# Transposes of the last two preparations moved to the DMA queue, their projections set two tiles behind the aggregation

## The chip, the cores and the metric

One core of one Trainium2 chip runs the whole program in one launch. The metric is the device time in microseconds. Three runs of the kernel before took 705.76, 706.26 and 706.27 us; the median is 706.26.

## The reference

Four layers on 2048 nodes with 256 features and one 0/1 adjacency matrix. Each layer's result is added to its input and normalised per row (mean and variance over the 256 features).

```python
x = layernorm(x + adj @ (x @ W0) + b0)
# attention, 4 heads: e = leaky_relu(src_i + dst_j) + adj;  att = softmax(e)
x = layernorm(x + mean_heads(att @ (x @ W1)))
# two convolutions: conv(x) = relu(x @ Wa + adj @ (x @ Wb) + b)
h = conv1(x);  x = layernorm(x + relu(conv2(h) + h))
# graph convolution: relu(adj_norm @ x @ W3), adj_norm = d^-1/2 (adj + I) d^-1/2
x = layernorm(x + relu(adj_norm @ (x @ W3)))
```

## The kernel before

Rows are handled in T = 16 tiles of P = 128; D = 256. Every float32 operand of TensorE is split into two float16 parts, hi and lo, and a product is made of such parts: a projection is six matmuls (three pairs of parts, two halves of the contraction), an aggregation two per tile of columns (the adjacency is exact in bf16, the projected features have hi and lo).

There are five **preparations**, k = 0 to 4 (k = 0 the first layer, 1 the attention's sources, 2 and 3 the two convolutions, 4 the graph convolution), and four **aggregations**, a = 0 to 3, for k = 0, 2, 3, 4. While aggregation a runs, preparation of the next k is woven into it. This text speaks of k = 3 woven into a = 1 ("convolution 2") and k = 4 woven into a = 2 ("the graph convolution"). A preparation of a tile goes through all engines:

- VectorE, `stages`: sum of the aggregated tile out of PSUM (line 779; 776 in the last aggregation), for k = 4 also residual, statistics (793, 800, 804), normalise (759); then `split` writes the hi part into the ring `xs` of R = 4 slots (827 for k = 3, 829 for k = 4).
- GpSimd: for k = 4 the inverse deviation (1109, 1111); `prep_lo` writes the lo part (1116).
- The tile is turned. Tiles 0 to 10 (`EARLY` = 11) by a DMA transpose that SP issues (lines 292 to 298; SP waits for each to land before the next, line 298). Tiles 11 to 15 by four TensorE transposes (`transpose`, 504) into the banks 4 and 5 of PSUM, evacuated by ScalarE (336).
- TensorE, `project` (541): six matmuls into bank 6 or 7 (`prep_bank`), 512 columns wide for k = 3, 256 for k = 4.
- ScalarE, `take_p`: the hi part of the projected features into `pset` (345; for k = 4 also 344). VectorE, `take`: lo part and own term (741, 744).

The order on TensorE is written out by hand. An aggregation works the row tiles 0 to 3 in four banks together (`group0`), then the tiles 4 to 15 one after the other (`rest`, lines 586 to 602): 16 steps j of two matmuls (550 hi, 551 lo) into one bank. Round t of `rest` first waits for the sum four tiles back (591). The projection of tile t - 5 of the next preparation is put ahead of step j = 14 of tile t. After the last tile, `tail` (604 to 614) does the transposes 11 to 15 and the projections 11 to 15, between pieces of the next aggregation's `group0`.

The order on VectorE is `first_sums` (tiles 0 to 3) and `other_sums` (835 to 877). Round t of `other_sums` interleaves the early stages of tile t (sum first) with the late ones of tile t - 1 (normalise, split), then the take of tile t - 4. So the split of tile t - 1 always stands behind the sum of tile t.

```python
                for n in range(max(len(early), len(late_))):
                    for st in early[n:n + 1] + late_[n:n + 1]:
                        st()
```

`pset` holds hi and lo of every tile in rows of PW = D + 2 float16: 1032 bytes to a tile, lo at byte 516, and hi's column D is the column of ones that gives the degrees in a = 0. The attention's `val` has rows of the same PW per head and tile, hi and lo in two arrays, which the change leaves alone.

Of the kernel before, what the change touches and what calls it, by code (L numbers as in the profile page):

```python
# [7 lines left out]
def graph_stack(nc, x_in, adj_in, w0_in, b0_in, w1_in, a_in, w2a_in, b1_in, w2b_in, b2_in, w3_in, out):  # L8
# [23 lines left out]
    R = 4  # L32
# [19 lines left out]
    with ctx:  # L52
# [62 lines left out]
        PSET = T * 2 * PW // 2  # L115
        pset = [part(arena, (s * PSET, (s + 1) * PSET), F16, "p (t q f) -> p t q f", t=T, q=2) for s in range(2)]
# [39 lines left out]
        s_td = sem("s_td")  # L156
# [57 lines left out]
        EARLY = T - R - 1  # L214

        def by_pe(k, t):

            return k * T + t if k < 2 else 2 * T + (k - 3) * (T - EARLY) + t - EARLY

        def conv_turned(t):  # L220

            return s_tc[t % 2], 16 * (t // 2 + 1)

        def prep_bank(k, u):

            return ps[:, 4 + u if k == 2 else 6 + u % 2, :]

        def by_dma(k, t):

            return 16 * ((k - 3) * EARLY + t + 1)  # L230

# [5 lines left out]
        def _(sp):  # L237
# [43 lines left out]
            for t in range(T):  # L281
                if t >= 2:
                    sp.wait_ge(*conv_turned(t - 2))
                if t % R == 0:
                    if t // R < SLOTS - 1:
                        sp.wait_ge(s_mm, (GROUPS - 1) * (T - 1) + T - SLOTS + t // R + 1)
                    else:
                        sp.wait_ge(s_z, GROUPS * BANKS)
                sp.wait_ge(s_lo, 2 * T + t + 1)
                sp.dma_start_transpose(xt[:, t, :].rearrange("p (c i) -> p c i", c=2 * K2),  # L290
                                       xs[:, t % R, :, :].rearrange("p q f -> p (q f)")).then_inc(s_tc[t % 2], 16)
            for k in (3, 4):
                sp.wait_ge(s_w, k * T)
                for t in range(EARLY):
                    sp.wait_ge(s_lo, k * T + t + 1)
                    sp.dma_start_transpose(xt[:, t, :].rearrange("p (c i) -> p c i", c=2 * K2),
                                           xs[:, t % R, :, :].rearrange("p q f -> p (q f)")).then_inc(s_td, 16)
                    sp.wait_ge(s_td, by_dma(k, t))
# [20 lines left out]
        def _(act):  # L319
# [6 lines left out]
            def split_hi(k, t, u, src, ready):  # L326
                ready(act)
                if k == 2 and t >= R:
                    act.wait_ge(*conv_turned(t - R))
                elif k == 0 and t >= R:  # L330
                    act.wait_ge(s_t, t - R + 1)
# [6 lines left out]
            def take_p(k, t, u):  # L338
                act.wait_ge(s_w, t + (k * T + 1))
                b = prep_bank(k, u)  # L340
                dst = pset[k % 2][:, at(t, 1), 0, 0:D].rearrange("p a f -> p (a f)")
# [148 lines left out]
            for k in (3, 4):  # L490
                tiles(act, 0, EARLY - EARLY % R, lambda t, u: take_p(k, t, u))
                for t in range(EARLY - EARLY % R, EARLY):
                    take_p(k, t, t % R)
                lagged(k, EARLY)
# [3 lines left out]
        def _(pe):  # L498
# [11 lines left out]
            def project(k, t, u):  # L510
                if k == 0 and isinstance(t, int) and t == 0:
                    pe.wait_ge(s_wl, 1)
                if k == 2:
                    pe.wait_ge(*conv_turned(t))
                elif k > 2 and not (isinstance(t, int) and t >= EARLY):
                    pe.wait_ge(s_td, by_dma(k, t))
# [4 lines left out]
                elif k == 2:  # L521
# [23 lines left out]
            def agg_step(a, k, it, bank, j, done):  # L545
# [4 lines left out]
                nc.tensor.matmul(ps[:, bank, 0:width], lhs, pp[:, j, 0, 0:width], start=(j == 0), stop=False)  # L550
                ins = nc.tensor.matmul(ps[:, bank, 0:D], lhs, pp[:, j, 1, 0:D], start=False, stop=(j == T - 1))  # L551
# [34 lines left out]
            def rest(a, knext, ready):  # L586
# [3 lines left out]
                def one(t, u):  # L590
                    pe.wait_ge(s_sum, t + (a * T - R + 1))
                    prep = knext is not None and not (isinstance(t, int) and t == R)
                    for j in range(T):
# [4 lines left out]
                        if j == (T - 2 if knext in (3, 4) else T // 2 + 2) and prep:  # L598
                            project(knext, t - R - 1, (u - 1) % R)
                        agg_step(a, k, t, u, j, j == T - 1)  # L600
                one(R, 0)
                tiles(pe, R + 1, T, one)

            def tail(k, a):

                e = T - R
# [578 lines left out]
```

## Time and profile before

| | us |
|---|---|
| runs, median (lowest to highest) | 706.26 (705.76 to 706.27) |
| the profiled execution | 704.71 |
| its span | 702.6 |
| mean granted clock of TensorE | 0.999 |
| TensorE busy | 686.1 (98%) |
| VectorE busy | 527.8 (75%) |
| ScalarE busy | 393.6 (56%) |
| GpSimd busy | 148.7 (21%) |

By stage, in us from the span's start: the first layer and the attention's set-up to about 134, the attention to 472, preparation k = 2 with its first sums to 507, a = 1 with k = 3 to 585, a = 2 with k = 4 to 654, a = 3 to the end. Times in the profile are microseconds unless marked ns. PE is TensorE, PEld its weight load, DVE VectorE, ACT ScalarE, POOL GpSimd, SP the queue that issues DMAs; a q behind the name is the engine's sequencer, L541 is line 541. A matmul's duration holds the way through the array, so the distance from one start to the next is its cost. `ring_hl` is the buffer that the turned tiles `xt` lie in, `ring_a` that of `xs`, `arena` holds `pset`, own and hidden terms.

### The profile page before, as it was taken

How to read it: one execution, taken by the hardware profiler on the slowest of the kernel's cores; microseconds unless marked ns; L12 is line 12 of the kernel's file. 1: busy time of each engine (PE TensorE's matmuls, PEld its weight loads, DVE VectorE, ACT ScalarE, POOL GpSimd, SP SyncE). 2: the span in 40 equal slices, each digit the busy share in tenths (PEclk: the TensorE clock that was granted, in tenths of full speed). 3: DMA queues.
4: the chain of work that ended last, by engine and by line, in shares of the span. 5: the costliest groups of instructions: out<-in, count | busy, mean ns of one | idle time of the engine just before them, and what ended most of it. 6: DMA issues, size and time to landing. Idle time of an engine off the chain costs nothing.

```text
span 702.6 us, 16657 instructions
## 1 busy us (share of the span) xinstructions
PE 686.1 (98%) x5962; PEld 567.2 (81%) x5962; DVE 527.8 (75%) x985; ACT 393.6 (56%) x525; POOL 148.7 (21%) x239
## 2 busy tenths in 40 slices
PE   6989999999999999999999999999999999999996
PEld 4878854688888888888888888876677778888885
DVE  5888646999898989989899898998432325874564
ACT  7554146888989889798898989643100020223000
POOL 4966422000100000000000000654011102432222
PEclk9999999999999999999999999999999999999999
DMA  8986001000303012030300303013121000210011
GB/s 327 413 311 261 0 3 60 1 1 31 62 31 61 0 42 49 30 60 0 80 10 30 60 0 60 2 29 70 23 46 31 8 1 16 39 30 2 31 49 42
DMA packets 33147, 42.17 MB, mean 60 GB/s; under 512 B 21776, under 2 KB 27856, under 8 KB 30928
## 3 DMA queue, kind: packets, MB, share of 16 engines
q1 hardware_dynamic: 30528, 33.73, 14.7%
q0 software_dynamic: 2016, 7.34, 5.6%
q8 instruction: 28, 0.46, 0.3%
q10 hardware_dynamic: 560, 0.52, 0.2%
q14 instruction: 15, 0.12, 0.1%
HBM read 27.13 MB, written 2.13 MB: 42 GB/s over the span
## 4 chain that ended last, share of the span: by engine, by line
PE 89%; DVE 7%; ACT 1%; issue 1%; DMA 1%; POOL 1%; DVEq 0%; SPq 0%; POOLq 0%; ACTq 0%
PE ps L550 15%; PE ps L551 15%; PE ps L692 14%; PE ps L694 14%; PE ps L693 14%; PE ps L541 9%; PE ps L642 5%; DVE ring_hl L986 2%; DVE ring_a L981 2%; PE ps L504 1%; DMA x<-in_x 1%; DVE x L759 1%; POOL ring_a L1116 0%; DVE stat L753 0%; PE ps L533 0%
## 5 line engine op out<-in xcount | busy, mean ns | idle before, releaser
L694 PE MATMUL ps<-arena,ring_hl 128*128 (+1 forms) x1024 | 279.6, 273 | 0.0
L692 PE MATMUL ps<-arena,ring_hl 128*128 (+1 forms) x1024 | 278.9, 272 | 0.4 <-DVE ring_hl L986 0.4
L693 PE MATMUL ps<-arena,ring_hl 128*128 (+1 forms) x1024 | 278.6, 272 | 0.0
L550 PE MATMUL ps<-arena,adj 128*128 128x256 f16 (+1 forms) x1024 | 230.5, 272 | 0.5 <-issue 0.5
L551 PE MATMUL ps<-arena,adj 128*128 128x256 f16 x1024 | 230.6, 273 | 0.0
L981 DVE SCALAR_TENSOR_TENSOR ring_a<-rho,gam,ring_a 128x1024 f32<-128x1024 f32 x128 | 163.8, 1280 | 18.0 <-ACT ring_a L435 18.0
L986 DVE TENSOR_TENSOR ring_hl<-ring_a,ring_hl 128x1024 f16<-128x1024 f32 x128 | 156.6, 1223 | 6.0 <-ACT ring_hl L449 5.9
L449 ACT ACTIVATE ring_hl<-ring_a 128x1024 f16<-128x1024 f32 x128 | 135.2, 1056 | 44.3 <-PE ps L694 31.0
L435 ACT ACTIVATE ring_a<-adj,shift 128x1024 f32<-128x1024 bf16 x128 | 145.6, 1138 | 0.0
L550 PEld LDWEIGHTS ps<-arena,adj 128*128 (+1 forms) x1024 | 99.9, 98 | 18.2 <-issue 0.7
L551 PEld LDWEIGHTS ps<-arena,adj 128*128 (+1 forms) x1024 | 99.5, 97 | 16.1
L692 PEld LDWEIGHTS ps<-arena,ring_hl 128*128 128x128 f16 x1024 | 100.0, 98 | 12.8 <-DVE ring_hl L986 0.9
L693 PEld LDWEIGHTS ps<-arena,ring_hl 128*128 128x128 f16 x1024 | 99.1, 97 | 13.7
L694 PEld LDWEIGHTS ps<-arena,ring_hl 128*128 128x128 f16 x1024 | 99.5, 97 | 13.1
L1139 POOL DMA_DIRECT2D x<-y x14 | 12.3, 880 | 308.3 <-ACT y L464 308.3
L345 ACT ACTIVATE arena<-ps 128x256 f16<-128x256 f32 (+1 forms) x48 | 18.5, 385 | 96.1 <-PE ps L541 95.8
L741 DVE SCALAR_TENSOR_TENSOR arena<-ps,w 128x256 f32<-128x256 f32 (+1 forms) x32 | 13.5, 422 | 56.1 <-ACT arena L345 56.0
L336 ACT ACTIVATE ring_hl<-ps 128x512 f16<-128x512 f16 (+1 forms) x42 | 25.0, 597 | 42.0 <-PE ps L504 42.0
L1111 POOL TENSOR_TENSOR rstd<-veps,neghalf 128x1 f32<-128x1 f32 x64 | 44.5, 696 | 5.0
L642 PE MATMUL ps<-w,ring_hl 128*128 128x512 f16 x192 | 42.7, 379 | 0.6 <-DVE arena L964 0.6
L1116 POOL TENSOR_TENSOR ring_a<-x,ring_a 128x256 f16<-128x256 f16 (+1 forms) x38 | 31.9, 842 | 43.4 <-DVE ring_a L829 39.9
L759 DVE TENSOR_SCALAR x<-total,mv,rstd 128x256 f32<-128x256 f32 (+1 forms) x48 | 19.8, 411 | 26.3 <-POOL rstd L1111 26.3
(91 smaller groups left out, 553.7 us busy)
## 6 DMA issues: line engine op xcount, KB each, us to landing
arena<-in_adj SPq DMA_DIRECT2D x16, 1024.0 KB, 9.1
x<-y POOLq DMA_DIRECT2D x14, 512.0 KB, 5.2
rho<-s_scratch SPq DMA_DIRECT2D x8, 512.0 KB, 3.7
out_x<-x SPq DMA_DIRECT2D x16, 128.0 KB, 1.7
x<-in_x SPq DMA_DIRECT2D x3, 512.0 KB, 6.9
arena<-in_L_gnn_W SPq DMA_DIRECT2D x1, 1024.0 KB, 16.4
arena<-in_L_gnn_a SPq DMA_DIRECT2D x1, 1024.0 KB, 19.4
rho<-in_L_gnn_W SPq DMA_DIRECT2D x2, 512.0 KB, 10.4
```

Source lines behind the costliest of these rows:

```text
L435: nc.scalar.activation(ring_a[:, jt % SLOTS, :], adj[:, jt, q * CH:(q + 1) * CH], ACT.Exp, bias=shift[:, at(h, 1), jt]).then_inc(s_e, 1)
L449: nc.scalar.activation(ring_hl[:, jt % SLOTS, 0], ring_a[:, jt % SLOTS], ACT.Copy).then_inc(s_ah, 1)
L541: ins = nc.tensor.matmul(bank[:, 0:width], xpart(a, kk), w[:, b, kk, :], start=(n == 0), stop=(n == len(steps) - 1))
L550: nc.tensor.matmul(ps[:, bank, 0:width], lhs, pp[:, j, 0, 0:width], start=(j == 0), stop=False)
L551: ins = nc.tensor.matmul(ps[:, bank, 0:D], lhs, pp[:, j, 1, 0:D], start=False, stop=(j == T - 1))
L642: ins = nc.tensor.matmul(ps[:, 2 * u + half, :], xtt[:, (a * K2 + kk) * P:(a * K2 + kk + 1) * P], w1[:, b, kk, half * 512:(half + 1) * 512 ...
L692: nc.tensor.matmul(acc, hi, v_hi, start=(jt == 0), stop=False)
L693: nc.tensor.matmul(ps[:, b, 0:D], hi, v_lo, start=False, stop=False)
L694: ins = nc.tensor.matmul(acc, lo, v_hi, start=False, stop=(jt == T - 1))
L981: nc.vector.scalar_tensor_tensor(a, rho[:, q, :], gam[:, at(h, 1), jt], a, op0=ALU.max, op1=ALU.mult)\
L986: nc.vector.tensor_sub(ring_hl[:, jt % SLOTS, 1], ring_a[:, jt % SLOTS], ring_hl[:, jt % SLOTS, 0])\
L1111: nc.gpsimd.tensor_tensor(rstd[:, slot:slot + 1], veps[:, slot:slot + 1], neghalf[:, 0:1], ALU.pow)\
```

## The change

All 16 tiles of k = 3 and 4 are turned by DMA, two semaphores in turn as k = 2 already had them, SP waiting for the landing two tiles back. A projection of k > 1 uses banks 4 to 7 and waits for the take four tiles back. The places of the projections on TensorE (tile: projected tile, step j) and of the takes on VectorE are written in two tables; from tile 9 (k = 3) and 13 (k = 4) on, tile t projects tile t - 2 at j = 14. The tail has two projections and no transposes. `rest` and `other_sums` are unrolled for these preparations instead of looping from tile 8. The rows of `pset` are 2 x 264 + 2 x 256 = 1040 bytes, lo at byte 528.

```diff
 
-        PSET = T * 2 * PW // 2
-        pset = [part(arena, (s * PSET, (s + 1) * PSET), F16, "p (t q f) -> p t q f", t=T, q=2) for s in range(2)]
+        LOW = D + 8
+        PSET = T * (LOW + D) // 2
+        pset = [part(arena, (s * PSET, (s + 1) * PSET), F16, "p (t f) -> p t f", t=T) for s in range(2)]
...
 
-        EARLY = T - R - 1
-
...
 
-            return k * T + t if k < 2 else 2 * T + (k - 3) * (T - EARLY) + t - EARLY
-
-        def conv_turned(t):
-
-            return s_tc[t % 2], 16 * (t // 2 + 1)
+            return k * T + t
+
+        def turned(k, t):
+
+            return s_tc[t % 2], 16 * ((k - 2) * T // 2 + t // 2 + 1)
+
+        PLACES = {3: {5: [(0, T - 2)], 6: [(1, 2), (2, T - 2)], 7: [(3, 2), (4, T - 2)], 8: [(5, 2), (6, T - 2)],
+                      **{t: [(t - 2, T - 2)] for t in range(9, T)}},
+                  4: {5: [(0, T - 2)], 6: [(1, T - 2)], 7: [(2, T - 2)], 8: [(3, JH), (4, T - 2)], 9: [(5, T - 2)],
+                      10: [(6, JH), (7, T - 2)], 11: [(8, T - 2)], 12: [(9, JH), (10, T - 2)],
+                      **{t: [(t - 2, T - 2)] for t in range(13, T)}}}
+        TAKES = {3: {5: [0], 6: [1, 2], 7: [3, 4], 8: [5, 6], **{t: [t - 2] for t in range(9, T)}},
+                 4: {4: [0], 5: [1], 6: [2, 3], 7: [4, 5], **{t: [t - 2] for t in range(8, T)}}}
...
 
-            return ps[:, 4 + u if k == 2 else 6 + u % 2, :]
-
-        def by_dma(k, t):
-
-            return 16 * ((k - 3) * EARLY + t + 1)
+            return ps[:, 4 + u if k > 1 else 6 + u % 2, :]
...
 
-            for t in range(T):
-                if t >= 2:
-                    sp.wait_ge(*conv_turned(t - 2))
-                if t % R == 0:
-                    if t // R < SLOTS - 1:
-                        sp.wait_ge(s_mm, (GROUPS - 1) * (T - 1) + T - SLOTS + t // R + 1)
-                    else:
-                        sp.wait_ge(s_z, GROUPS * BANKS)
-                sp.wait_ge(s_lo, 2 * T + t + 1)
-                sp.dma_start_transpose(xt[:, t, :].rearrange("p (c i) -> p c i", c=2 * K2),
-                                       xs[:, t % R, :, :].rearrange("p q f -> p (q f)")).then_inc(s_tc[t % 2], 16)
-            for k in (3, 4):
-                sp.wait_ge(s_w, k * T)
-                for t in range(EARLY):
+            for k in (2, 3, 4):
+                if k > 2:
+                    sp.wait_ge(s_w, k * T)
+                for t in range(T):
+                    if t >= 2:
+                        sp.wait_ge(*turned(k, t - 2))
+                    if k == 2 and t % R == 0:
+                        if t // R < SLOTS - 1:
+                            sp.wait_ge(s_mm, (GROUPS - 1) * (T - 1) + T - SLOTS + t // R + 1)
+                        else:
+                            sp.wait_ge(s_z, GROUPS * BANKS)
...
                     sp.dma_start_transpose(xt[:, t, :].rearrange("p (c i) -> p c i", c=2 * K2),
-                                           xs[:, t % R, :, :].rearrange("p q f -> p (q f)")).then_inc(s_td, 16)
-                    sp.wait_ge(s_td, by_dma(k, t))
+                                           xs[:, t % R, :, :].rearrange("p q f -> p (q f)")).then_inc(s_tc[t % 2], 16)
...
                     pe.wait_ge(s_wl, 1)
-                if k == 2:
-                    pe.wait_ge(*conv_turned(t))
-                elif k > 2 and not (isinstance(t, int) and t >= EARLY):
-                    pe.wait_ge(s_td, by_dma(k, t))
+                if k > 1:
+                    pe.wait_ge(*turned(k, t))
...
                     pe.wait_ge(s_ev, BANKS * (GROUPS - 1) + 1 + t)
-                elif k == 2:
+                elif k > 1:
...
                 lhs = adj[:, j, at(it * P, P)]
-                nc.tensor.matmul(ps[:, bank, 0:width], lhs, pp[:, j, 0, 0:width], start=(j == 0), stop=False)
-                ins = nc.tensor.matmul(ps[:, bank, 0:D], lhs, pp[:, j, 1, 0:D], start=False, stop=(j == T - 1))
+                nc.tensor.matmul(ps[:, bank, 0:width], lhs, pp[:, j, 0:width], start=(j == 0), stop=False)
+                ins = nc.tensor.matmul(ps[:, bank, 0:D], lhs, pp[:, j, LOW:LOW + D], start=False, stop=(j == T - 1))
...
                             transpose(knext, t - R - 1, (u - 1) % R)
-                        if j == (T - 2 if knext in (3, 4) else T // 2 + 2) and prep:
+                        if j == T // 2 + 2 and prep and knext < 3:
                             project(knext, t - R - 1, (u - 1) % R)
+                        for n, place in PLACES.get(knext, {}).get(t, []) if isinstance(t, int) else []:
+                            if place == j:
+                                project(knext, n, n % R)
...
                 one(R, 0)
-                tiles(pe, R + 1, T, one)
+                if knext in PLACES:
+                    for t in range(R + 1, T):
+                        one(t, t % R)
+                else:
+                    tiles(pe, R + 1, T, one)
...
 
-                e = T - R
-                plan = [([], e - 1, None), ([0, 1, 2], e, e - 1), ([3, 4], e + 1, e), ([5, 6], e + 2, e + 1),
-                        ([7, 8], e + 3, e + 2), ([9, 10], None, e + 3), (list(range(11, T)), None, None)]
-                for js, tt, tp in plan:
+                for js, tp in ((range(0, 5), T - 2), (range(5, 10), T - 1), (range(10, T), None)):
                     group0(a, k, js)
-                    if tt is not None:
-                        transpose(k, tt, tt % R)
...
                         dve.wait_ge(s_t, t + (k * T - R + 1))
-                    elif k == 3 and isinstance(t, int) and t < R:
-                        dve.wait_ge(*conv_turned(t + T - R))
-                    elif isinstance(t, int) and (t < R or t >= EARLY + R):
-                        dve.wait_ge(s_t, by_pe(*((k, t - R) if t >= R else (k - 1, t + T - R))) + 1)
+                    elif t < R:
+                        dve.wait_ge(*turned(k - 1, t + T - R))
                     else:
-                        dve.wait_ge(s_td, by_dma(k, t - R))
+                        dve.wait_ge(*turned(k, t - R))
...
                             lines[t][s - (t - 1)]()
-                for n, st in enumerate(lines[3][1:]):
-                    if n + 1 == len(lines[3]) - len(stages(a, k, 3, 3)[1]) and k is not None:
-                        take(k, 0, 0)
+                for st in lines[3][1:]:
...
                         late_ = []
-                    if k is not None and not (isinstance(t, int) and t == R and a > 0):
+                    if k == 1:
                         late_.append(lambda: take(k, t - R, u))
+                    for n in TAKES[k].get(t, []) if k in TAKES else []:
+                        late_.append(lambda n=n: take(k, n, n % R))
...
                             st()
-                peeled = max(len(fill), 1)
+                peeled = T - R if k in TAKES else max(len(fill), 1)
...
                 if k is not None:
-                    for t in range(T - R, T):
+                    for t in range(T - (R if k == 1 else 2), T):
```

Not shown: the same change of names and indices in ScalarE's `split_hi` and `take_p`, in VectorE's `take` and in GpSimd's memset of the ones; ScalarE's part for k = 3 and 4 becomes a loop of `take_p` over the 16 tiles.

## Rows read from the trace of the kernel before

**Rows 1.** The page's busy times: engine, us, share of the span, instructions.

```profile
PE 686.1 (98%) x5962; PEld 567.2 (81%) x5962; DVE 527.8 (75%) x985; ACT 393.6 (56%) x525; POOL 148.7 (21%) x239
```

**Rows 2.** The chain of waits in convolution 2: start us, us, what.

```profile
528.31 1.29 PE ps L541 x6
...
533.14 1.29 PE ps L541 x6
```

**Rows 3.** The timeline of two tile starts, last aggregation: start us, us, engine, line.

```profile
679.07 0.27 PE L550 MATMUL ps<-arena,adj 128*128 128x256 f16 x1
...
679.50 0.48 DVE L776 SCALAR_TENSOR_TENSOR arena<-ps,dis,arena 128x256 f32 x1 [1.70 <-PE ps L551]
...
682.60 0.27 PE L550 MATMUL ps<-arena,adj 128*128 128x256 f16 x1
```

**Rows 4.** The chain of waits, a tile turned on TensorE in the tail.

```profile
566.70 0.22 PE ps L504 x4
```

**Rows 5.** The timeline of one preparation in convolution 2, DVE, POOL and SP.

```profile
526.02 0.41 DVE L779 TENSOR_TENSOR arena<-ps,arena 128x256 f32<-128x256 f32 x1
526.35 0.28 DVE L827 TENSOR_SCALAR ring_a<-arena 128x256 f16<-128x256 f32 x1
...
526.83 0.67 POOL L1116 TENSOR_TENSOR ring_a<-arena,ring_a 128x256 f16<-128x256 f16 x1 [4.15 <-DVE ring_a L827]
527.57 1.19 SPq L296 DMA_TRANSPOSE ring_hl<-ring_a  x1
```

**Rows 6.** The chain of waits, graph convolution's first projection.

```profile
590.11 2.43 DMA ring_hl<-ring_a
...
592.58 0.83 PE ps L541 x6
```

**Rows 7.** The timeline of DVE and POOL in the graph convolution's preparation.

```profile
598.99 0.41 DVE L779 TENSOR_TENSOR arena<-ps,arena 128x256 f32<-128x256 f32 x1
...
618.84 0.41 DVE L759 TENSOR_SCALAR x<-total,mv,rstd 128x256 f32 x1 [0.47 <-POOL rstd L1111]
...
621.01 0.18 DVE L804 BATCH_NORM_AGGREGATE mv<-stat 128x2 f32<-128x6 f32 x1
...
622.12 0.41 DVE L759 TENSOR_SCALAR x<-total,mv,rstd 128x256 f32 x1 [0.47 <-POOL rstd L1111]
622.44 0.42 DVE L786 SCALAR_TENSOR_TENSOR arena<-arena  x1
622.78 0.41 DVE L829 TENSOR_SCALAR ring_a<-total,mv,rstd 128x256 f16<-128x256 f32 x1
...
623.38 0.67 POOL L1116 TENSOR_TENSOR ring_a<-x,ring_a 128x256 f16<-128x256 f16 x1 [1.30 <-DVE ring_a L829]
```

**Rows 8.** The timeline of a projection and its takes, graph convolution.

```profile
600.97 0.82 PE L541 MATMUL ps<-w,ring_hl 128*128 128x256 f16 x6
601.62 0.27 PE L550 MATMUL ps<-arena,adj 128*128 128x256 f16 x1
...
602.01 0.47 ACT L344 ACTIVATE arena<-ps,dis2w 128x256 f32 x1 [3.35 <-PE ps L541]
602.38 0.47 ACT L345 ACTIVATE arena<-ps,disw 128x256 f32 x1
...
631.50 0.47 ACT L345 ACTIVATE arena<-ps,disw 128x256 f16<-128x256 f32 x1
...
632.27 0.48 DVE L744 SCALAR_TENSOR_TENSOR arena<-ps,disw,arena 128x256 f32 x1 [0.81 <-ACT arena L345]
```

**Rows 9.** The 22 transposes of line 296, issue to landing.

```profile
DMA to landing us min/median/max: 2.4/2.4/4.3
```

**Rows 10.** Busy times by stretch, the attention's head 0 and head 2: us (matmuls).

```profile
150.00:200.00 50.00, 50.00 (x458) 44.58 (x456) 46.10 (x47) 43.74 (x48) 2.04 (x2) 1.00 0.15 33
...
300.00:350.00 50.00, 50.00 (x459) 44.20 (x457) 43.72 (x53) 44.23 (x54) 3.44 (x4) 1.00 0.21 44
```

**Rows 11.** Busy times by stretch, first layer: stretch, length, PE first, PEclk third last.

```profile
42.00:50.00 8.00, 5.74 (x59) 4.84 (x57) 6.69 (x18) 2.87 (x4) 5.74 (x7) 1.00 0.69 253
```

More of the change, by code:

```diff
@@ L155, in graph_stack @@
         s_t, s_xt = sem("s_t"), sem("s_xt")
-        s_td = sem("s_td")
         s_tc = [sem(f"s_tc{i}") for i in range(2)]
@@ L328, in split_hi @@
                 if k == 2 and t >= R:
-                    act.wait_ge(*conv_turned(t - R))
+                    act.wait_ge(*turned(2, t - R))
                 elif k == 0 and t >= R:
@@ L340, in take_p @@
                 b = prep_bank(k, u)
-                dst = pset[k % 2][:, at(t, 1), 0, 0:D].rearrange("p a f -> p (a f)")
+                dst = pset[k % 2][:, at(t, 1), 0:D].rearrange("p a f -> p (a f)")
                 src = b[:, D:2 * D] if k in (2, 3) else b[:, 0:D]
@@ L490, in _ @@
             for k in (3, 4):
[L491 to L494, printed above, removed]
+                tiles(act, 0, T, lambda t, u: take_p(k, t, u))
         @block.tensor
@@ L736, in take @@
                 dve.wait_ge(s_ph, t + ((k - (k > 1)) * T + 1))
-                hi = pset[k % 2][:, at(t, 1), 0, 0:D].rearrange("p a f -> p (a f)")
-                lo = pset[k % 2][:, at(t, 1), 1, 0:D].rearrange("p a f -> p (a f)")
+                hi = pset[k % 2][:, at(t, 1), 0:D].rearrange("p a f -> p (a f)")
+                lo = pset[k % 2][:, at(t, 1), LOW:LOW + D].rearrange("p a f -> p (a f)")
                 ot = tile_of(own, t)
@@ L1073, in _ @@
             nc.gpsimd.memset(ident[:, :], 0.0).then_inc(s_id0, 1)
-            nc.gpsimd.memset(pset[0][:, :, 0, D:D + 1], 1.0).then_inc(s_one, 1)
+            nc.gpsimd.memset(pset[0][:, :, D:D + 1], 1.0).then_inc(s_one, 1)
             pool.wait_ge(s_id0, 1)
```

## The prediction, made before the result was known

> **What bounds the kernel now.** I read the page's busy times first. TensorE is busy 98% of the span [rows 1]. Then the chain of waits in the stretch the diff touches: convolution 2 and the graph convolution, some 507 to 654 us. It is TensorE alone, tile after tile, 4.83 us apart in convolution 2 [rows 2]; a tile without a projection takes 682.60 - 679.07 = 3.53 us for its 32 aggregation matmuls, 16 pairs of 0.22 [rows 3], so a convolution projection costs 1.30, and one of the graph convolution 601.62 - 600.97 = 0.65 [rows 8]. TensorE has next to no idle time to win there. What can be won is work taken off it; what can be lost is a new wait. So I asked of each moved projection when its transposed tile lands.
>
> **What is taken off.** Before, tiles 11 to 15 of both preparations are turned on TensorE: four transposes to a tile, 40 in all. Four take 0.22 us of the chain [rows 4], so ten tiles give back 2.2 us. ScalarE loses ten evacuations; it isn't on the chain and this is worth nothing. Ten more transposes go to SP's queue, 1.19 us each to issue [rows 5]; tiles come over 4 us apart, the queue hides them, and SP's next work, the output stores, comes only in the last aggregation. Four banks instead of two: a projection waits for the take four tiles back, which VectorE has long made; worth nothing, and without that slack the second projection of tiles 6 to 8 would wait for the first one's take, some 1.5 us behind it [rows 8]. The old tail began each bank of the next layer with 3 rows, the new one with 5, so its fourth bank asks for the last sum later: I give that 0.4 us, one VectorE sum.
>
> **The chain that the new places make, convolution 2.** Call E the moment TensorE begins tile t. VectorE's round t-1 begins with the sum of tile t-1, which waits for the aggregation that ended at E; the split of tile t-2 stands behind that sum. So the tile that is projected in tile t can't be split before E. Step by step:
> - TensorE's new tile to VectorE's sum: 679.50 - 679.07 = 0.43 [rows 3].
> - Sum to split: 526.35 - 526.02 = 0.33; split to GpSimd's low part: 0.48; that to SP's issue: 0.74 [rows 5].
> - Issue to landing 2.43, landing to first matmul 0.04 [rows 6].
>
> The sum is 4.45 us after E. TensorE gets to place 14 after 14 pairs, 14/16 of 3.53 = 3.09 us. It waits 1.36 us, and since the aggregation's last two pairs are queued behind the wait, the tile's sum, VectorE's next round and the next tile start late too: nothing of it is caught up. Tiles 9 to 15 have this form: 7 x 1.36 = 9.5 us. Tiles 5 to 7 project what was split a round earlier and wait for nothing; tile 8 projects two, 3.09 + 1.30 = 4.39, and waits 0.1. In the tail, tile 14 comes after 20 pairs (4.41), just in time.
>
> **The same for the graph convolution.** Here the split is preceded by sum, normalise and max. VectorE's steps follow at 0.32 to 0.34 us (622.12, 622.44, 622.78), GpSimd starts 0.60 after the split [rows 7]. Chain: 0.43 + 0.33 + 0.32 + 0.34 + 0.60 + 0.74 + 2.43 + 0.04 = 5.23 us. Against 3.09 that is 2.14 for each of tiles 13, 14, 15: 6.4 us; in the tail 5.23 - 4.41 = 0.8.
>
> Earlier tiles depend on VectorE's lag. It comes out of its first four tiles late: it sums tile 4 at 598.99, when TensorE is near the end of tile 7 (600.97, rows 8). Its rounds are 622.12 - 618.84 = 3.28 us against TensorE's 3.53 + 0.65, so it gains 0.9 us a tile [rows 7]. I walked the two queues tile by tile with the steps above. Tile 8's second projection waits 0.3. The largest wait is tile 10: round 7 takes tile 5, whose projection stands at the end of tile 9. The take is ready 0.39 + 0.37 + 0.77 = 1.53 us after that projection ends [rows 8], or 1.09 after tile 10 starts (two pairs, 0.44, lie between). Only then come the take (0.48) and tile 7's statistics end; tile 7's normalise follows them by 622.12 - 621.01 = 1.11 [rows 7], its split by another 0.66, and 3.81 more to the matmul: 7.15 us after E (1.09 + 0.48 + 1.11 + 0.66 + 3.81). TensorE wants it at 3.09 + 0.65 = 3.74: 3.4 us of wait. The same walk gives 1.5 and 2.2 for the two projections of tile 12. Together 0.3 + 3.4 + 3.7 + 6.4 + 0.8 = 14.6 us.
>
> **Long landings.** The transposes land in 2.4 us in the middle and 4.3 at most [rows 9]. Until now a late one was covered by three tiles of lag; on this path it is paid in full. Bounds for the 15 awaited ones: none late, 0; all late, 15 x 1.9 = 28. Nearest is the median, so I take two late ones at 1.2: 2.3 us.
>
> **Padding.** The row of a tile goes from 1032 to 1040 bytes, the low half from byte 516 to 528. No row prices this. From above: six projection matmuls, whose operand rows start at multiples of 512 bytes, take 0.65 us, 109 ns each [rows 8], and an aggregation matmul 3.53/32 = 110.3 [rows 3]; if the padding brings one to the other, 2048 x 1.4 = 2.9 us. From below: in the attention head 0's value rows start at a multiple of 16 bytes and head 2's eight bytes past one, and 50 us hold 458 and 459 matmuls [rows 10]: nothing. A loss isn't excluded but no row hints at one: it adds no instruction. I take a gain of 1.7, because in the waiting tiles all but the last two pairs only lengthen the wait.
> The Trainium skill, SBUF — State Buffer, Specifications (TRN2), says that SBUF has 16-byte lines and that each cross to a new line pays a penalty; a 512-byte row off a line touches 33 of them instead of 32, which by that rule would be up to 3% of the aggregations, an estimated 7 us. The attention's two counts speak against it.
>
> **The sum.** Gains 2.2 + 0.4 + 1.7 = 4.3; losses 9.6 + 14.6 + 2.3 = 26.5; net +22.2. The profiled execution took 704.71 us (span 702.6, 2.1 around it), the median of the runs is 706.26, 1.55 above it; I add the net to the median: **728.5 us**.
>
> **Rivals.**
> - *The waits aren't there, faster.* For it: the rest of VectorE, GpSimd and SP is idle enough, and if the chain of steps were under 3.09 us the lag of two tiles would hide it all. Against: issue to landing alone is 2.43. Then 706.3 - 4.3 = 702.0. It decides for "faster" when the chain is below 3.09 us in convolution 2 and the last rounds of the graph convolution. Chance 0.07.
> - *Only the steady waits.* VectorE's lag falls otherwise than I walked it, and tiles 8, 10 and 12 of the graph convolution wait for little: 706.3 + 9.6 + 7.2 + 2.3 - 4.3 = 721.1. For it: that walk has the most steps. Chance 0.10.
> - *The clock falls.* TensorE would be idle about a fifth of these stretches. If its clock dropped to 1.2 GHz through 13 waiting tiles, the 3.09 before the projection becomes 6.18, which is 1.7 past the chain, and the 1.74 of work after it doubles: (1.7 + 1.7) x 13 = 45 us more, 773. Against: in the stretch 42 to 50 us TensorE is idle 2.26 of 8 us, 28% of it, and the clock still reads 1.00 [rows 11]. Chance 0.04.
> The Trainium skill, TensorE: Matmul & The Clock Gate, HAM oscillation, describes such a kernel, whose short bursts between waits on DMA each start at the low clock; this trace has no fallen clock beside such a gap.
> - *Gains and waits cancel*, within 0.2% of 706.3 (about 1.4 us, what a measurement of this kernel can tell from no change): it needs a chain some 1.2 us shorter and tile 10 without its wait. Chance 0.02.
>
> **How the numbers follow.** The forecast has 0.77. Its own bounds are 0 to 6 us of late landings, 0 to 2.9 of padding, and one or two us either way in the walk: about 723 to 734. To hold 8 in 10 I reach down to the steady-waits case: 719 to 735. Left out are the faster case, the cancelling case, the clock case and what is outside the bounds. Faster 0.07, same 0.02, slower 0.91.
>
> **What the profile would show.** TensorE's idle time before the projection's matmuls, released by the DMA ring_hl<-ring_a: about 26 us in some 17 waits, seven of them 1.4 us in convolution 2 and four about 2.1 in the graph convolution, one over 3; tiles 6.2 us apart in convolution 2. VectorE's sum 0.4 us behind each TensorE tile. No L504 after 100 us. The aggregation's 32 matmuls in 3.48 us if the padding tells, 3.53 if not. The forecast is wrong if the projection finds its tile landed, that is if the distance from a tile's start to the landing is under 3.1 us.

## The result and the profile after

The changed kernel takes **727.48 us** (median of 4 runs, 727.36 to 728.70) where the kernel before takes 706.11: a ratio of 1.0313 [1.0301, 1.0326] (in brackets the 95% interval). The ratio is the one on record; the quotient of the two medians is 1.0303. Below too the two differ by up to 0.001, so about 0.7 us of any difference between two versions hangs on which is taken. It was forecast slower, at 728.5 in a range of 719 to 735. The profiled execution took 727.37 us, its span is 724.9, 22.3 more than before. The page, busy times first, then the chain of waits by engine and line:

```profile
span 724.9 us, 16115 instructions
PE 687.5 (95%) x5922; PEld 566.3 (78%) x5922; DVE 526.9 (73%) x985; ACT 388.8 (54%) x515; POOL 148.9 (21%) x239
PE 78%; DVE 10%; DMA 6%; POOL 3%; issue 2%; ACT 1%; POOLq 0%; SPq 0%; ACTq 0%; DVEq 0%
```

TensorE has 40 matmuls fewer than in [rows 1] and is busy 95% instead of 98%; DMA now has 6% of the chain. Who waited for whom between 500 and 680 us (us in total, times, longest):

```profile
PEld ps L534 <- DMA ring_hl<-ring_a: 24.6, 16, 3.6
PE ps L534 <- DMA ring_hl<-ring_a: 20.1, 16, 3.3
```

L534 is the projection. Its weight load waits 24.6 us for transposes to land, in 16 waits. (The matmul's own figure is smaller because the array is still draining for part of the time. In the rest of the text a wait is the distance between two matmul starts less the 0.11 us of the first.) One tile of convolution 2, from the timeline; columns as in [rows 3]:

```profile
538.50 1.47 PE L534 MATMUL ps<-w2b,ring_hl 128*128 128x512 f16 x6 [1.00 <-DMA ring_hl<-ring_a]
...
540.24 0.27 PE L543 MATMUL ps<-arena,adj 128*128 128x256 f16 x1
...
540.44 0.42 DVE L774 TENSOR_TENSOR arena<-ps,arena 128x256 f32<-128x256 f32 x1 [3.81 <-PE ps L544]
...
540.78 0.28 DVE L820 TENSOR_SCALAR ring_a<-arena 128x256 f16<-128x256 f32 x1
...
541.26 0.67 POOL L1109 TENSOR_TENSOR ring_a<-arena,ring_a 128x256 f16<-128x256 f16 x1 [5.29 <-DVE ring_a L820]
...
542.00 1.19 SPq L295 DMA_TRANSPOSE ring_hl<-ring_a  x1
...
544.45 1.47 PE L534 MATMUL ps<-w2b,ring_hl 128*128 128x512 f16 x6 [0.99 <-DMA ring_hl<-ring_a]
```

```profile
542.00 2.40 DMA ring_hl<-ring_a
544.41 0.05 issue
```

This is the chain of the prediction, link by link (the second fence is the same tile in the chain of waits). The tile starts at 540.24, VectorE's sum follows 0.20 later, the split 0.34, the low part 0.48, the issue 0.74, the landing 2.40, the matmul 0.04: 4.21 us. TensorE was there after 3.06 (14 pairs of 0.218). Projections are 544.45 - 538.50 = 5.95 us apart where it was 4.83 [rows 2]. Seven such waits measure 1.15 to 1.17 us each. VectorE is idle 3.81 us before its sum: it is not short of time, it stands in the wrong place of its queue.

### The profile page after: what moved, and what is told of

Read it like the earlier page. It is cut to its first block, busy times and chain, and to the rows that moved or that the text cites. A ratio compares the mean times of both kernels' runs of the same rounds, so it can differ in the third digit from the quotient of the medians.

```text
span 724.9 us, 16115 instructions
## 1 busy us (share of the span) xinstructions
PE 687.5 (95%) x5922; PEld 566.3 (78%) x5922; DVE 526.9 (73%) x985; ACT 388.8 (54%) x515; POOL 148.9 (21%) x239
## 4 chain that ended last, share of the span: by engine, by line
PE 78%; DVE 10%; DMA 6%; POOL 3%; issue 2%; ACT 1%; POOLq 0%; SPq 0%; ACTq 0%; DVEq 0%
PE ps L687 14%; PE ps L689 14%; PE ps L688 14%; PE ps L543 11%; PE ps L544 11%; PE ps L534 9%; PE ps L637 5%; DMA ring_hl<-ring_a 5%; DVE ring_hl L979 2%; DVE ring_a L974 2%; POOL ring_a L1109 2%; DVE x L754 1%; PE ps L499 1%; POOL rstd L1104 1%; DVE arena L781 1%
## 5 line engine op out<-in xcount | busy, mean ns | idle before, releaser
L543 PEld LDWEIGHTS ps<-arena,adj 128*128 128x128 bf16 (+1 forms) x1024 | 100.7, 98 | 17.5 <-issue 0.9
L544 PEld LDWEIGHTS ps<-arena,adj 128*128 128x128 bf16 (+1 forms) x1024 | 100.8, 98 | 15.1
L774 DVE TENSOR_TENSOR arena<-ps,arena 128x256 f32<-128x256 f32 x32 | 13.2, 414 | 65.1 <-PE ps L544 65.1
L342 ACT ACTIVATE arena<-ps,dis2w 128x256 f32 x16 | 7.6, 473 | 71.1 <-PE ps L534 71.1
L534 PE MATMUL ps<-w,ring_hl 128*128 128x256 f16 x192 | 29.3, 294 | 14.4 <-DMA ring_hl<-ring_a 12.9
```

The costliest lines, as they stand in the source:

```text
L534: ins = nc.tensor.matmul(bank[:, 0:width], xpart(a, kk), w[:, b, kk, :], start=(n == 0), stop=(n == len(steps) - 1))
L543: nc.tensor.matmul(ps[:, bank, 0:width], lhs, pp[:, j, 0:width], start=(j == 0), stop=False)
L544: ins = nc.tensor.matmul(ps[:, bank, 0:D], lhs, pp[:, j, LOW:LOW + D], start=False, stop=(j == T - 1))
```

## Experiments

Each ratio is to the kernel before, run on the same chip beside it (it took 705.1 to 705.8 us there). Each diff is against the changed kernel unless it says otherwise, and is cut to the lines that matter: where places move, takes and tail move with them. The record also has the mean granted clock of every execution, a share of the full one: 0.991 to 0.994 in the four of the changed kernel, 0.996 to 0.999 in those of the kernel before beside the experiments. So a difference in time can be one of clock.

**1. Padding alone.** The kernel before with rows of 1040 bytes.

```diff
-        PSET = T * 2 * PW // 2
+        ROW = 2 * (D + 8) - 8
+        PSET = T * ROW // 2
...
-                ins = nc.tensor.matmul(ps[:, bank, 0:D], lhs, pp[:, j, 1, 0:D], start=False, stop=(j == T - 1))
+                ins = nc.tensor.matmul(ps[:, bank, 0:D], lhs, pp[:, j, D + 8:2 * D + 8], start=False, stop=(j == T - 1))
```

> The kernel before with the feature rows padded to 1040 bytes and nothing else. If the start of a row matters to TensorE (the changed kernel's trace has an aggregation pair at 0.218 to 0.219 us where the kernel before has 0.2205), the 1024 pairs save about 1.5 to 2.5 us: 703.6 to 704.6. If that difference comes from somewhere else in the change, the time stays within 0.3 us of 706.1.

Measured: 703.60 us, ratio 0.9978 [0.9965, 0.9990]: 1.5 us less. Busy times in a stretch of the last aggregation, matmuls in brackets behind PE; first the kernel before, then this one:

```profile
658.00:693.00 35.00, 35.00 (x320) 30.83 (x318) 20.30 (x73) 0.00 (x0) 9.60 (x26) 1.00 0.15 50
```

```profile
658.00:693.00 35.00, 35.00 (x323) 31.36 (x322) 20.08 (x73) 0.00 (x0) 9.60 (x26) 1.00 0.15 50
```

323 matmuls in place of 320 in 35 us. Over all starts of one pair behind another in the last three aggregations, a matmul costs 109.2 ns instead of 110.4, in the first 109.8 instead of 111.6. So the padding does speed TensorE, by 1536 x 1.2 + 512 x 1.8 ns = 2.8 us of work. The 1.5 us measured is less, with an interval of 0.7 to 2.5; the profiled execution also had a stretch of fallen clock (below), which takes about as much away as is missing. But the kernel before has executions with a lower clock too (on average it reads 0.998, this version 0.997), so the clock can be a part of the reason only, as far as is shown.

**2. All tiles by DMA, old places.** The two tables, the tail and the rows as before; transposes, banks and unrolling as in the change.

```diff
+        PLACES = {3: {t: [(t - 5, T - 2)] for t in range(5, T)},
+                  4: {t: [(t - 5, T - 2)] for t in range(5, T)}}
+        TAKES = {3: {t: [t - 4] for t in range(4, T)},
+                 4: {t: [t - 4] for t in range(4, T)}}
```

> The changed kernel with every projection and take put back where the kernel before has them (five tiles behind, five projections in the tail), unpadded rows; all tiles are still turned by DMA, four banks, rounds unrolled. If the new waits alone make the change slow: 706.1 less the 2.2 us of transposes, 703.5 to 704.3, with no TensorE wait for a transpose but the first of the graph convolution (0.6 us). If the ten more DMA transposes, the unrolled code or the banks cost something by themselves, it stays above 706.

Measured: 703.54 us, ratio 0.9977 [0.9966, 0.9987], 1.6 us less; the 2.2 us of transposes lie within it. TensorE waits for a transpose once, as in the kernel before:

```profile
PEld ps L536 <- DMA ring_hl<-ring_a: 0.7, 1, 0.7
```

So turning by DMA, four banks and unrolled rounds cost nothing that shows. What made the change slow is in the two tables with their tail (the rows aren't it: experiment 6 has the new rows and is as fast).

**3. Convolution 2 three tiles behind**, the graph convolution as changed.

```diff
-                      **{t: [(t - 2, T - 2)] for t in range(9, T)}},
+                      **{t: [(t - 3, T - 2)] for t in range(8, T)}},
...
-                for js, tp in ((range(0, 5), T - 2), (range(5, 10), T - 1), (range(10, T), None)):
+                for js, tp in TAIL[k]:
...
+        TAIL = {3: [(range(0, 5), T - 3), (range(5, 8), T - 2), (range(8, 11), T - 1), (range(11, T), None)],
```

> The changed kernel with convolution 2 alone projected three tiles behind (three projections in the tail); the graph convolution keeps its places. A tile more of lag gives the chain 4.8 us more, over the 1.36 it lacks: its seven waits of 1.27 and the 0.5 in the tail go, 727.5 - 9.4 = 718.1, and the graph convolution's waits stay at about 14. If the waits only move to other projections, less than 3 us is won.

Measured: 717.22 us, ratio 1.0181 [1.0161, 1.0201]: 1.3% of 706, 9.3 us, less than the changed kernel. The waits of convolution 2 make 8.6 us of it. Part of the rest can be clock: this version's executions take 715.3 and 716.5 us at a granted clock of 0.999 and 0.996, 718.0 and 719.8 at 0.991. The waits for transposes:

```profile
PEld ps L537 <- DMA ring_hl<-ring_a: 15.8, 9, 3.2
```

Nine instead of 16. The eight left besides the first projection's are the graph convolution's, and they stand as walked: tile 8, 10, 12 (two), 13, 14, 15 and the tail, here the timeline from tile 10 on.

```profile
617.16 0.83 PE L537 MATMUL ps<-w,ring_hl 128*128 128x256 f16 x6 [2.95 <-DMA ring_hl<-ring_a]
...
625.53 0.83 PE L537 MATMUL ps<-w,ring_hl 128*128 128x256 f16 x6 [1.21 <-DMA ring_hl<-ring_a]
...
629.61 0.83 PE L537 MATMUL ps<-w,ring_hl 128*128 128x256 f16 x6 [1.94 <-DMA ring_hl<-ring_a]
...
635.71 0.83 PE L537 MATMUL ps<-w,ring_hl 128*128 128x256 f16 x6 [1.78 <-DMA ring_hl<-ring_a]
641.82 0.83 PE L537 MATMUL ps<-w,ring_hl 128*128 128x256 f16 x6 [1.78 <-DMA ring_hl<-ring_a]
647.93 0.83 PE L537 MATMUL ps<-w,ring_hl 128*128 128x256 f16 x6 [1.79 <-DMA ring_hl<-ring_a]
654.03 0.83 PE L537 MATMUL ps<-w,ring_hl 128*128 128x256 f16 x6 [0.47 <-DMA ring_hl<-ring_a]
```

By distance of starts the eight are 1.06, 3.11, 1.37, 2.10, 1.95, 1.94, 1.95 and 0.63 us, 14.1 together.

**4. The graph convolution five tiles behind**, convolution 2 as changed.

```diff
-                  4: {5: [(0, T - 2)], 6: [(1, T - 2)], 7: [(2, T - 2)], 8: [(3, JH), (4, T - 2)], 9: [(5, T - 2)],
...
+                  4: {6: [(0, 4), (1, T - 2)], **{t: [(t - 5, T - 2)] for t in range(7, T)}}
```

> The changed kernel with the graph convolution alone put back to five tiles behind, its first projection a little later still; convolution 2 keeps two tiles. Its waits (some 14 us by the steps, 0.8 of them at the first projection) go: 727.5 - 14.4 = 713.1, less up to 1 us more if the two stretches at the low clock, which lie in this stage, go too. Convolution 2 still waits seven times 1.27 us. If VectorE's lag were the limit rather than the places, TensorE would wait for the same landings later and the time would stay over 720.

Measured: 710.48 us, ratio 1.0086 [1.0065, 1.0107], 16.0 us under the changed kernel. Its waits make 14.3 of that: the 14.1 of experiment 3, and 0.2 at the first projection, which waits 0.5 instead of 0.7. The changed kernel's two stretches of fallen clock (2.7 us, below) lie in this stage, and this trace has none there; that would make 17.0, within the interval of 1.5 us either way. Convolution 2 keeps seven waits of 1.15 to 1.17 us and one of 0.6 in the tail; the graph convolution has one of 0.5 left. With experiment 3, 9.3 + 16.0 = 25.3 us: that is the whole loss of 22.1 us and 3.2 more, about what the version of experiment 5 gains.

**5. Both.** Places of experiments 3 and 4 together, padded rows.

> The changed kernel with both preparations on places that the steps say need no wait: convolution 2 three tiles behind, the graph convolution five behind with its first projection at tile 6; all tiles by DMA, rows padded. If the waits are the whole loss and the three gains add up: before, less 2.2 (transposes), less some 2 (padding; it alone measured -1.5), less 0.4 to 1.0 (first wait of the graph convolution): a ratio to the kernel before of 0.992 to 0.995, 699.5 to 701.5 us where the kernel before takes 705.1. If something else of the change costs, it is over 702.

Measured: 702.04 us, ratio 0.9946 [0.9928, 0.9963], 3.8 us faster than the kernel before. The interval lies wholly under 1. The 702.04 us touch the 702 over which another cost was expected, but the kernel before took 705.83 beside them, not 705.1; the ratio is inside the expected range.

**6. Five behind in both, padded rows**: experiment 2 with the rows of the change.

> All tiles by DMA, every projection five tiles behind as in the kernel before, rows padded: the transposes' gain (0.9977 by itself) and the padding's (0.9978 by itself) together. If they add, 0.9955. Against the version with three and five tiles of lag (0.9946) it lacks only the 0.6 us at the first projection of the graph convolution and the 0.4 us behind the last sum, so 0.9955 to 0.9960. If the two gains overlap (both shorten TensorE's path, so they should not), it is over 0.997.

Measured: 702.15 us, ratio 0.9948 [0.9931, 0.9966]. The two gains add (0.9977 x 0.9978 = 0.9955, inside the interval). That it stands level with experiment 5 means that the half us at the graph convolution's first projection, and the one behind the last sum, can't be seen in the time.

**7. Split before the sum.** Two tiles behind as in the change; on VectorE, in convolution 2 alone, the split of tile t - 1 goes ahead of the sum of tile t.

```diff
-                        for st in early[n:n + 1] + late_[n:n + 1]:
+                        pair = (early[n:n + 1], late_[n:n + 1])
+                        for st in sum(pair[::-1] if k == 3 and n == 0 else pair, []):
```

> The changed kernel, projections still two tiles behind; only on VectorE in convolution 2, a round splits tile t-1 before the sum of tile t instead of behind it. If the queue order on VectorE is what ties the chain to the tile's start, the split comes a whole tile earlier, the seven waits of 1.27 us and the 0.5 behind them go and the ratio falls from 1.031 to about 1.018, as with three tiles of lag. If the distance from split to landing (3.7 us) alone were the cause, the waits would stay.

Measured: ratio 1.0188 [1.0173, 1.0203], as with three tiles of lag. VectorE's timeline shows the split (L820) done and the sum (L774) waiting behind it, and the projections 4.79 us apart:

```profile
541.72 0.28 DVE L820 TENSOR_SCALAR ring_a<-arena 128x256 f16<-128x256 f32 x1
...
543.25 1.46 PE L534 MATMUL ps<-w2b,ring_hl 128*128 128x512 f16 x6
...
545.18 0.42 DVE L774 TENSOR_TENSOR arena<-ps,arena 128x256 f32<-128x256 f32 x1 [3.18 <-PE ps L544]
...
548.04 1.46 PE L534 MATMUL ps<-w2b,ring_hl 128*128 128x512 f16 x6
```

Nothing changed but this order, and 8.8 us (1.25% of 706) are gone. So the lag of two tiles wasn't too short for the chain of split, low part and landing; it was too short for that chain behind a sum.

**8. Takes in step** with the projections, graph convolution.

```diff
-                 4: {4: [0], 5: [1], 6: [2, 3], 7: [4, 5], **{t: [t - 2] for t in range(8, T)}}}
+                 4: {5: [0], 6: [1], 7: [2, 3], 8: [4], 9: [5], 10: [6, 7], 11: [8], 12: [9, 10],
+                     **{t: [t - 2] for t in range(13, T)}}}
```

> The changed kernel, only VectorE's takes of the graph convolution moved one to three rounds later, into the round of the tile that projects them (take 5 from round 7 to 9). If take 5 holding round 7 makes the 3.3 us wait at tile 10, that wait falls to about 1.2, the 1.5 at tile 12's first projection goes and the 2.2 at its second falls to 1.5; the others stay: 4.7 us less, a ratio of about 1.025. If VectorE's own load makes these waits, they stay as they are.

Measured: ratio 1.0207 [1.0193, 1.0222], 7.5 us under the changed kernel (6.5 by the medians) where 4.7 were expected. The waits did what was said: 3.1 us fell to 1.17, 1.4 went, 2.1 fell to 1.28, the others of this stage stayed.

```profile
626.65 0.83 PE L535 MATMUL ps<-w,ring_hl 128*128 128x256 f16 x6 [1.00 <-DMA ring_hl<-ring_a]
...
630.81 0.82 PE L535 MATMUL ps<-w,ring_hl 128*128 128x256 f16 x6
...
633.64 0.82 PE L535 MATMUL ps<-w,ring_hl 128*128 128x256 f16 x6
...
636.89 0.28 PE L535 MATMUL ps<-w,ring_hl 128*128 128x256 f16 x1 [1.11 <-DMA ring_hl<-ring_a]
```

Summed, that is 4.1 us. The rest is near what the fallen clock takes from the changed kernel in this stage (below); this trace has none there, and the four executions read 0.995 to 0.998. The trace also has a wait of 1.5 us in convolution 2's tail where the changed kernel's has 0.45, behind a transpose that took 4.06 us to land; it is the slowest of the four. That this accounts for all of it is argued, not shown.

**9. Place 10 instead of 14**, convolution 2.

```diff
-                      **{t: [(t - 2, T - 2)] for t in range(9, T)}},
+                      **{t: [(t - 2, T - 6)] for t in range(9, T)}},
```

> The changed kernel, only the projections of convolution 2 from tile 9 on put ahead of step 10 instead of 14. The landing is tied to the tile's start, so TensorE waits 0.88 us longer in each of seven tiles (2.15 instead of 1.27) and does 4 pairs more behind the projection: 6.1 us more, a ratio of 1.040. If the waits were a matter of how much the queues or TensorE have to do, the place would matter little and the time stays within 1 us of the changed kernel.

Measured: ratio 1.0379 [1.0360, 1.0397], 4.7 us over the changed kernel where 6.1 were expected. In the stage itself the expectation holds: seven waits of 2.04 us, projections 565.52 - 558.68 = 6.84 us apart, against 5.95: 0.89 a tile.

```profile
558.68 1.47 PE L534 MATMUL ps<-w2b,ring_hl 128*128 128x512 f16 x6 [1.88 <-DMA ring_hl<-ring_a]
...
565.52 0.82 PE L534 MATMUL ps<-w2b,ring_hl 128*128 128x512 f16 x3 [1.88 <-DMA ring_hl<-ring_a]
```

Again the graph convolution shows no fallen clock in this trace, which the changed kernel's does.

**10. The change without padding.**

```diff
-        LOW = D + 8
+        LOW = PW
```

> The changed kernel with the rows as before, 1032 bytes. The aggregation matmul goes back from 109.2 to 110.4 ns, but in the ten waiting tiles all but the last two pairs are covered by the wait; what is paid is 0.4 us in the two stages, 0.5 in the last aggregation and 1.0 in the first: 1.9 us more than the changed kernel, a ratio of 1.034. If the padding were worth its full 2.8 us here too, 1.035; if nothing, 1.031.

Measured: ratio 1.0303 [1.0277, 1.0329]. That is no slower than the changed kernel's 1.0313, and 1.034 lies outside the interval: the expectation was missed. (By the medians this version is 22.1 us over the kernel before, the changed one 21.4.) In the trace the aggregation matmul is back at 110.4 ns and the seven waits are 0.03 us shorter, so what padding wins ahead of a wait the wait takes back. From the tail's wait to the end of the span, a stretch without any wait for a transpose, it takes 59.3 us instead of 58.9. The clock blurs the rest. Two executions of this version have 726.45 us at a granted clock of 0.998 and 0.999, the other two 729.07 at 0.993 and 729.18 at 0.991. The changed kernel's four are all at 0.991 to 0.994 and take 727.4 to 728.7. At like clock this version is 0.5 to 1.7 us slower, so the medians don't exclude the forecast 1.9 as clearly as the interval says; so few executions don't settle it.

**11 and 12. Where a row starts.** Padding alone again, rows of 1040 bytes, one profiled execution each. Both diffs are against experiment 1. In 11 the low half starts at byte 516; in 12 the low half at 8 and the high half at 520.

```diff
-                ins = nc.tensor.matmul(ps[:, bank, 0:D], lhs, pp[:, j, D + 8:2 * D + 8], start=False, stop=(j == T - 1))
+                ins = nc.tensor.matmul(ps[:, bank, 0:D], lhs, pp[:, j, D + 2:2 * D + 2], start=False, stop=(j == T - 1))
```

```diff
-                nc.tensor.matmul(ps[:, bank, 0:width], lhs, pp[:, j, 0:width], start=(j == 0), stop=False)
-                ins = nc.tensor.matmul(ps[:, bank, 0:D], lhs, pp[:, j, D + 8:2 * D + 8], start=False, stop=(j == T - 1))
+                nc.tensor.matmul(ps[:, bank, 0:width], lhs, pp[:, j, D + 4:D + 4 + width], start=(j == 0), stop=False)
+                ins = nc.tensor.matmul(ps[:, bank, 0:D], lhs, pp[:, j, 4:D + 4], start=False, stop=(j == T - 1))
```

> Padding alone, rows of 1040 bytes, but the low half at byte 516, four past a multiple of 16. In the kernel before, tiles j with hi at 0 and lo at 4 bytes past a multiple of 16 start their pair 0.2165 us apart and those with 8 and 12 past 0.225. If only 8 and 12 cost, every aggregation matmul takes 109.2 ns on average here, as with all rows at 0. If any start off a multiple costs, it takes about 109.8, halfway to the 110.4 of the kernel before.

> Padding alone, rows of 1040 bytes, the low half first at byte 8, the high half at byte 520: every operand row starts eight past a multiple of 16. If a start eight past costs by itself, an aggregation matmul takes 111 ns or more (the pairs of odd j before: 112.5). If the cost is in going from one start to another, or is none as in the attention's head 2, it takes 109.2.

Both have 323 matmuls in the stretch of experiment 1 and a mean of 109.2 ns, like rows at multiples of 16, though 12 has all its rows eight past one. First 11, then 12:

```profile
658.00:693.00 35.00, 35.00 (x323) 31.37 (x322) 20.35 (x73) 0.00 (x0) 9.62 (x26) 1.00 0.15 50
```

```profile
658.00:693.00 35.00, 35.00 (x323) 30.95 (x321) 20.34 (x73) 0.00 (x0) 9.61 (x26) 1.00 0.15 50
```

A start four or eight bytes past a multiple of 16 costs nothing here by itself. Taken by tile of columns in the last aggregation, a pair of matmuls costs 218.3 ns in even and odd tiles alike in experiments 1 and 11. In the kernel before it costs 216.4 in even ones (starts 0 and 4 past) and 224.8 in odd ones (8 and 12 past), in experiment 12, whose starts are all 8 past, 220.0 and 216.7. The Trainium skill, SBUF — State Buffer, Specifications (TRN2), has each cross to a new 16-byte line pay; by that, experiment 12's rows, which touch one line more, would be slower, and they aren't. In the first aggregation alone, whose high rows have 257 columns, 11 is slower than padding alone, 110.8 ns against 109.8. What the old layout of 1032 bytes does that these don't (a start twelve past, or the change from one start to the next) stays open.

## Why the prediction was right, and where it was not

**The bound and the new wait**: right. TensorE was the path, and the change put a wait for each landed tile on it. Experiments 3 and 4 take the waits away and with them the loss, experiment 7 shows that it hangs on the order of sum and split on VectorE, experiment 9 that it is tied to the tile's start.

**The chain of convolution 2**: right in form, 0.24 us too long. The step that was mis-sized is its first, tile start to sum: 0.43 us came from the last aggregation [rows 3], and it is 0.20 here. The wait is 1.16, not 1.36; the stage lost 8.1 us in seven waits and 0.45 in the tail, where 9.6 was forecast.

**The graph convolution**: forecast 0.3, 3.4, 1.5, 2.2, three of 2.1 and 0.8, 14.6 in all; without fallen clock they are 1.1, 3.1, 1.4, 2.1, three of 1.95 and 0.6, 14.1 in all (experiment 3). The only one off by more than 0.3 us is tile 8's. Experiment 8 shows that the long one came from the take that held VectorE's round, as the walk had it.

**Long landings**: 2.3 us were put in. The longest landing of the changed kernel's 32 took 3.2 us, not 4.3 as in [rows 9]:

```profile
DMA to landing us min/median/max: 2.4/2.4/3.2
```

One wait of the changed kernel's ends at a late landing, the 0.45 us in convolution 2's tail (first row); tile 8's ends at a usual one (second row) and is 1.06 to 1.09 us in all five padded traces with these places.

```profile
577.77 3.01 DMA ring_hl<-ring_a
...
612.01 2.41 DMA ring_hl<-ring_a
```

So 0.45 us is theirs, and it stands in the waits above. This term was 1.85 too large, and by chance: experiment 8's 4.06 us landing met the same wait. Four of the 32 took 2.8 to 3.2 us. Each of the four has a 16 KB fetch of instructions on another queue in its time, as have the four late ones of the kernel before (3.0 to 4.3 us). Here is the fetch beside the first row above, from the DMA queues between 577.7 and 580.8 us (packets, MB, share):

```profile
q8 instruction: 1, 0.02, 1.9%
```

One more transpose of the 32 has the end of such a fetch at its start and lands in 2.4. That the fetches make the others late isn't shown.

**The clock**: it had 0.04 as a rival and no term in the sum, and this is the step that failed. It did fall, twice for 3.4 us, each time at the end of one of the two longest waits (3.1 and 3.5 us; the second is tile 12's, in experiment 3's trace two waits of 1.4 and 2.1):

```profile
599.00:627.00 28.00, 23.67 (x215) 20.48 (x213) 19.57 (x67) 5.87 (x14) 10.95 (x24) 1.00 0.21 38
627.00:630.40 3.40, 3.40 (x19) 2.42 (x17) 1.30 (x5) 0.84 (x2) 0.80 (x3) 0.50 0.24 43
630.40:640.60 10.20, 6.91 (x63) 5.91 (x61) 5.02 (x17) 1.68 (x4) 3.03 (x7) 1.00 0.13 27
640.60:644.00 3.40, 3.37 (x16) 2.33 (x17) 1.02 (x4) 0.84 (x2) 0.00 (x0) 0.50 0.00 0
644.00:665.00 21.00, 16.25 (x146) 13.83 (x144) 9.65 (x35) 2.52 (x6) 5.66 (x12) 1.00 0.10 21
```

The clock stands third from the end: 0.50, the 1.2 GHz level, in the second and fourth stretch. From the first projection's wait to the tail's, this takes 665.34 - 599.51 = 65.8 us; in experiment 3, same places and no fallen clock, 653.29 - 590.13 = 63.2. So the clock cost 2.7 us in this execution, and the other three read no higher (0.991 to 0.993 against 0.994). It didn't stay down for the stage, as the rival had it. The rival's counter-argument, that a gap of 2.3 us left the clock at 1.00 [rows 11], was weak: in other executions that same gap is followed by 3.4 us at half clock.

**Gains**: transposes, 2.2 forecast, 1.6 [0.9 to 2.4] by themselves (experiment 2). Padding, 1.7 forecast for this kernel; alone 1.5 [0.7 to 2.5], inside the change not settled (experiment 10). The later wait for the last sum, 0.4 forecast: the kernel before waits 0.25 us there, at 638.01, and the changed kernel doesn't. I gave no more because the attention's rows showed nothing; that row could not speak for these, whose starts change from matmul to matmul.

The total came out 1.0 us from the forecast partly because errors cancel: waits with their late landings were put at 26.5 us and are 8.6 + 14.1 = 22.7, 3.8 too much, against 2.7 us of clock left out. That part is luck; the range holds without it.

## What to carry to other kernels

Before a consumer is moved nearer to its producer, add up the chain from the event that truly starts it, and that is not always the producer's own work: here an unrelated wait (the next tile's sum) stood ahead of the split in an in-order queue, and taking the split ahead of it is worth as much as a whole tile of lag. A wait on the bounding engine that recurs in every tile is paid in every tile. Distance cost nothing here: five tiles of lag in both preparations (experiment 6) are level with three and five (experiment 5). So take more lag than the chain needs, as long as buffers allow it. The best two versions measured keep the DMA transposes and the padding: 702.04 us, 0.9946 [0.9928, 0.9963] of the kernel before, with lags of three and five tiles, and 702.15 with five in both.

## What the runs showed of the hardware that was not expected

- **The same gap sometimes costs clock.** In the first layer TensorE stands idle 2.3 us from about 44 us on. Eight of the 14 traces then show 3.4 us at 1.2 GHz, 47.3 to 50.7 us here, others none. First padding alone, then the kernel before:

```profile
47.30:50.70 3.40, 3.40 (x24) 2.42 (x22) 2.77 (x7) 1.83 (x2) 2.37 (x4) 0.50 0.58 186
```

```profile
47.30:50.70 3.40, 3.40 (x39) 3.01 (x37) 2.91 (x7) 2.14 (x2) 2.45 (x3) 1.00 0.63 229
```

  24 matmuls instead of 39 in the same 3.4 us. Experiment 5's trace has two such stretches, at 18 us behind a gap of 1.8 and at 49, and a span of 701.2 us; that of experiment 6, level with it in time, has none and 697.9. The Trainium skill, TensorE: Matmul & The Clock Gate, HAM oscillation, tells of the clock falling at waits on DMA in every round; here seven waits of 1.2 us in a row, or seven of 2.0 (experiment 9), never brought it down, and waits of 3.1 us and more did in some executions only.
- **An aggregation matmul's cost hangs on the layout of its moving rows**, 110.4 against 109.2 ns, but not on their start in the simple way that padding to 16 bytes suggests (experiments 11 and 12).
